# The first layer norm's normalisation moved from VectorE to ScalarE, as a scale and a shift

## The chip, the cores and the metric

The kernel runs on one core of a Trainium2 chip. The metric is the device time of one execution in microseconds (us). The engines are TensorE (PE, and PEld for its weight loads), VectorE (DVE), ScalarE (ACT), GpSimd (POOL) and the sync engine (SP), which issues most DMAs. Each takes its own list of instructions in order, and they wait for one another with semaphores.

## The reference

One transformer layer on 2 x 1024 tokens of width 512, all in float32. Cut to what matters:

```python
def _layernorm(x, axis=-1, eps=1e-05):
    m = jnp.mean(x, axis=axis, keepdims=True)
    v = jnp.var(x, axis=axis, keepdims=True)
    return (x - m) / jnp.sqrt(v + eps)

x = _layernorm(x + attention(x))      # 16 heads of 32, low-rank additions to q, k, v, o
x = _layernorm(x + moe(x))            # 8 experts, the best one per token, capacity 256, and a shared expert
```

The change is in the first of the two layer norms, between the attention's output projection and the router and experts.

## The kernel before

The kernel computes float32 products as three products of a high and a low half (`hi`, `lo`), so every operand of TensorE is first split: ScalarE writes the high half (a rounding copy) and VectorE the rest (a subtraction).

The attention takes until about 634 us. Then comes the stage of the change, over 16 tiles of 128 tokens by 512, in four groups of four (`i`, with `t = 4*i + j`), and after it the shared expert, the routing and the experts.

For a tile t of this stage:

- SP loads the attention columns (`at_in`, L535) and the input rows (`xr`, L538). GpSimd adds the output bias to `xr` (L693).
- ScalarE makes the high half of `at_in` (`at_hi`, L1267), VectorE the low half (`at_rest`, L1548). TensorE multiplies with `Wo` (`project`, L993, which is recorded at L751).
- VectorE adds the residual to the product in `rows[:, t]` (L1587) and takes the statistics (L1591).
- After four tiles, VectorE aggregates and adds epsilon (L1568, L1570), ScalarE takes the root (`root`, L1291), and VectorE forms the reciprocal with one Newton step (`scales`, L1575 to L1579) and normalises the four tiles in place (L1627).
- TensorE transposes the four normalised tiles (`turn_x1`, L1001, recorded at L758), after the projection of the next group; ScalarE takes the high half of the transposed tile (`x1_hi`, L1167) and VectorE the rest (`x1_rest`, L1420).

The order is written out by hand in each engine's list. On VectorE a group i is: the four tiles, each with the low half for the tile two further on; aggregation; the rest of the transposed tiles of group i-1; the scales; the four normalisations; for i = 1, 2, 3 the low half of one chunk of the shared expert's weights (`conv(13, ...)`, L1601). On ScalarE a group i is: the high halves for tiles 4i+2 to 4i+5; a copy of logits for i = 2, 3; the high halves of the transposed tiles of group i-1; the root; for i = 1, 2, 3 the high half of that same chunk (L1300). On TensorE: the projection of the group, logits of group i-2 for i = 2, 3, the transposes of group i-1; at the end the transposes of group 3, then the first product of the shared expert. SP loads tiles in order, but has loads of weight chunks between them: before tile 12's columns it waits for the semaphore `conv13`, which VectorE's L1601 increments, and loads the chunk (13, 2).

The second layer norm, at the kernel's end, already works with a scale and a shift: VectorE computes them (L1749, L1750) and ScalarE applies them (L1387).

Of the kernel before, what the change touches and what calls it, by code (L numbers as in the profile page):

```python
# [23 lines left out]
F32 = mybir.dt.float32  # L24
# [3 lines left out]
ACT = mybir.ActivationFunctionType  # L28
ALU = mybir.AluOpType
AX = mybir.AxisListType  # L30

P = 128
# [200 lines left out]
def emit(nc, ctx, x, W, bias, bo, Bm, Am, Wg, W1, W3, W2, sw1, sw3, sw2, out):  # L233
    sems = {}

    def sem(name):
        if name not in sems:
            sems[name] = ctx.enter_context(nc.semaphore(name))
        return sems[name]
# [66 lines left out]
    early = Arena(nc, region, small_at - V_BYTES)  # L306
# [7 lines left out]
    wg_raw = early("wg_raw", [P, DC, E], F32)  # L314
    st6 = early("st6", [P, 4, 6], F32)
    mv = early("mv", [P, 4, 2], F32)
    ln_v, ln_s, ln_r, ln_t = (early(f"ln_{n}", [P, 4], F32) for n in "vsrt")
    mid = Arena(nc, small_at - V_BYTES, overlay)
    raw2 = [mid(f"raw2_{i}", [P, D], F32) for i in range(2)]
    r3 = {n: mid(f"r3_{n}", [P, NT, E], F32) for n in ("lg", "d", "ex", "c", "oh", "s0", "s1", "io")}  # L320
# [7 lines left out]
    ln2_v, ln2_s, ln2_r, ln2_t, ln2_scale, ln2_shift = (mid(f"ln2_{n}", [P, NT], F32) for n in ("v", "s", "r", "t", "scale", "shift"))  # L328
    gate_sb = mid("gate_sb", [P, E * CAP // P], F32)
    wide = Arena(nc, overlay, sum_at)  # L330
    rows = wide("rows", [P, NT, D], F32)
# [827 lines left out]
    def _(ac):  # L1159
        ACTV = nc.scalar.activation  # L1160
# [58 lines left out]
        i, dc = 4, 0  # L1219
# [42 lines left out]
        def at_hi(t):  # L1262

            ac.wait_ge(sem(f"at_ld{t % 4}"), t // 4 * 16 + 16)
            if t >= 2:
                ac.wait_ge(sem("o_full"), t - 1)
            ACTV(at[t % 2][0][:], at_in[t % 4][:], ACT.Identity).then_inc(sem("at_hi"), 1)  # L1267
# [13 lines left out]
        def x1_hi(i):  # L1281
            for j in range(4):
                turned(i, j, x1_bank(4 * i + j), ("x1_t", 0), "x1_hi")

        def take_logits(i):
            ac.wait_ge(sem("lg_full"), i + 1)
            ACTV(lgT[:, i * 512:(i + 1) * 512], bank[6 + i % 2][0:E, :], ACT.Copy).then_inc(sem("lg_ev"), 1)

        def root(k, name):
            ac.wait_ge(sem(name + "_var"), k)  # L1290
            ACTV(ln_s[:], ln_v[:], ACT.Sqrt).then_inc(sem(name + "_root"), 1)  # L1291


        def conv(kind, c, sets, need):

            if kind == 13:
                ac.wait_ge(sem(f"raw13_ld{c % 2}"), sets * 96 + 32 * (c // 2 + 1))
                if need is not None:
                    ac.wait_ge(sem("ab_full"), need + (c + 1))
                ACTV(w13[c][0][:], raw13[c % 2][:, 0:1 + (c < FC - 1)], ACT.Identity).then_inc(sem("conv13_hi"), 1)  # L1300
            else:
                ac.wait_ge(sem(f"raw2_ld{c % 2}"), sets * (8 * (6 + 2 * (c % 2))) + 16 * (c // 2 + 1 + (c == FC - 1)))
                if need is not None:
                    ac.wait_ge(sem("used2"), need + (c + 3))
                ACTV(w2[0][:, c], raw2[c % 2][:], ACT.Identity).then_inc(sem("conv2_hi"), 1)

        def step(c, q, width):

            r, p0 = c % 2, tail(c)
            ac.wait_ge(sem("ab_full"), q + (c + 1))  # L1310
            ac.wait_ge(sem("hid_lo"), q + (c + 1))
            ACTV(sa[r][p0:P, 0:width], bank[2 * r][0:P - p0, 0:width], ACT.Silu).then_inc(sem("sa_rdy"), 1)  # L1312
            ac.wait_ge(sem("h_done"), q + (c + 3))
            ac.wait_ge(sem("used2"), q + (c + 1))
            ACTV(hid[r][0][p0:P, 0:width], sa[r][p0:P, 0:width], ACT.Identity).then_inc(sem("hid_hi"), 1)  # L1315
# [21 lines left out]
        for i in range(4):  # L1337
            for t in range(4 * i + 2, min(4 * i + 6, NT)):
                at_hi(t)
            if i >= 2:  # L1340
                take_logits(i - 2)
            if i:
                x1_hi(i - 1)
            root(i + 1, "ln1")
            if i in FIRST_PROJ:
                conv(13, FIRST_PROJ[i], 0, None)
        x1_hi(3)
# [37 lines left out]
        def normalised(start, stop):  # L1385
            for t in range(start, stop):
                ACTV(rows[:, t], rows[:, t], ACT.Identity, scale=ln2_scale[:, t:t + 1],  # L1387
                     bias=ln2_shift[:, t:t + 1]).then_inc(sem("out_rdy"), 1)

        def root2(k, start, stop):  # L1390
            ac.wait_ge(sem("ln2_var"), k)
            ACTV(ln2_s[:, start:stop], ln2_v[:, start:stop], ACT.Sqrt).then_inc(sem("ln2_root"), 1)

        for c in range(FC):
            step(c, (E + 3) * FC, 512)
            if c == 3:
                root2(1, 0, 12)
            if c == 4:
                ac.wait_ge(sem("ln2_shift"), 1)
                normalised(0, 8)  # L1400
        normalised(8, 12)
        root2(2, 12, NT)
        ac.wait_ge(sem("ln2_shift"), 2)
        normalised(12, NT)


# [1 line left out]
    def _(ve):  # L1408
        TT, TS, RED = nc.vector.tensor_tensor, nc.vector.tensor_scalar, nc.vector.tensor_reduce
# [88 lines left out]
        n, i, t, dc = 0, 4, V_FIRST, 0  # L1498
# [66 lines left out]
        def variances(link, name):  # L1565

            for j in range(4):
                ins = nc.vector.bn_aggr(mv[:, j], st6[:, j])  # L1568
            link(ins)
            TS(ln_v[:], mv[:, :, 1], EPS, None, ALU.add).then_inc(sem(name + "_var"), 1)  # L1570

        def scales(link, k, name, out=ln_r):

            ve.wait_ge(sem(name + "_root"), k)
            link(nc.vector.reciprocal(ln_r[:], ln_s[:]))  # L1575
            link(TT(ln_t[:], ln_r[:], ln_r[:], ALU.mult))
            link(TT(ln_t[:], ln_t[:], ln_v[:], ALU.mult))
            link(TS(ln_t[:], ln_t[:], -0.5, 1.5, ALU.mult, ALU.add))
            link(TT(out[:], ln_r[:], ln_t[:], ALU.mult))  # L1579

        def tiles(i, link):

            for j in range(4):
                t = 4 * i + j
                ve.wait_ge(sem("o_full"), t + 1)
                ve.wait_ge(sem("xb_rdy"), t + 1)
                TT(rows[:, t], bank[(0, 1, 4)[t % 3]], xr[j][:], ALU.add).then_inc(sem("y_done"), 1)  # L1587
                if t + 2 < NT:
                    at_rest(t + 2)
                ve.wait_ge(sem("y_done"), t + 1)  # L1590
                link(nc.vector.bn_stats(st6[:, j], rows[:, t]))  # L1591

        def x1_rest(i):
            for j in range(4):
                turned(i, j, x1_bank(4 * i + j), "x1_hi", "x1_lo")

        def conv(kind, c, sets):

            if kind == 13:
                ve.wait_ge(sem("conv13_hi"), sets * FC + (c + 1))  # L1600
                TT(w13[c][1][:], raw13[c % 2][:, 0:1 + (c < FC - 1)], f32(w13[c][0][:]), ALU.subtract).then_inc(sem("conv13"), 1)  # L1601
            else:
                ve.wait_ge(sem("conv2_hi"), sets * FC + (c + 1))
                p0 = tail(c)
                TT(w2[1][p0:P, c], raw2[c % 2][p0:P, :], f32(w2[0][p0:P, c]), ALU.subtract).then_inc(sem("conv2"), 1)  # L1605
# [12 lines left out]
        link = Chain(ve, sem("ln1_chain"))  # L1618
        for i in range(4):
            tiles(i, link)  # L1620
            variances(link, "ln1")
            if i:
                x1_rest(i - 1)
            scales(link, i + 1, "ln1")
            for j in range(4):
                t = 4 * i + j
                TS(rows[:, t], rows[:, t], mv[:, j, 0:1], ln_r[:, j:j + 1], ALU.subtract, ALU.mult).then_inc(sem("x1_rdy"), 1)  # L1627
            if i in FIRST_PROJ:
                conv(13, FIRST_PROJ[i], 0)
        x1_rest(3)  # L1630
# [6 lines left out]
        def by_t(b, k=0):  # L1637
            return b[:, k * P:(k + 1) * P].rearrange("p (t e) -> p t e", e=E)

        link = Chain(ve, sem("rt_chain"))  # L1640
# [9 lines left out]
                                            op0=ALU.is_equal, op1=ALU.mult))  # L1650
# [12 lines left out]
        for k in (1, 2, 4, 8):  # L1663
# [9 lines left out]
                                            op0=ALU.mult, op1=ALU.add))  # L1673
# [53 lines left out]
        link = Chain(ve, sem("ln2_chain"))  # L1727
# [14 lines left out]
        def scales2(k, start, stop):  # L1742
            r, tt, v, scale = (x[:, start:stop] for x in (ln2_r, ln2_t, ln2_v, ln2_scale))
            ve.wait_ge(sem("ln2_root"), k)
            link(nc.vector.reciprocal(r, ln2_s[:, start:stop]))
            link(TT(tt, r, r, ALU.mult))
            link(TT(tt, tt, v, ALU.mult))
            link(TS(tt, tt, -0.5, 1.5, ALU.mult, ALU.add))
            link(TT(scale, r, tt, ALU.mult))  # L1749
            nc.vector.scalar_tensor_tensor(out=ln2_shift[:, start:stop], in0=mv2[:, start:stop, 0], scalar=-1.0, in1=scale,  # L1750
                                           op0=ALU.mult, op1=ALU.mult).then_inc(sem("ln2_shift"), 1)

        for c in range(FC):
            step(c, (E + 3) * FC, 512)
# [6 lines left out]
        for t in range(12, NT):  # L1761
# [4 lines left out]
            stats(t, t + 1)  # L1766
        variances2(12, NT)
        scales2(2, 12, NT)


# [32 lines left out]
```

## Time and profile before

| what | value |
|---|---|
| median of 3 runs | 1122.74 us (1121.78 to 1123.65) |
| the profiled execution, its own time | 1124.97 us |
| its span in the trace | 1123.3 us |
| PE busy | 1064.0 us (95%) |
| DVE busy | 725.5 us (65%) |
| ACT busy | 552.1 us (49%) |
| POOL busy | 472.9 us (42%) |

The span is what the trace covers; the device time has 1.7 us around it. Busy times are sums over the engine's instructions. In the rows of a timeline, the first two numbers are the start and the duration in us, and brackets at the end give how long the engine had been idle and what released it. A row with "x4" merges four instructions of one line.

### The profile page before, as it was taken

The page shows a single profiled execution, that of the slowest core. Times are in us where ns is not written, and L with a number is a line of the kernel's source. Part 1 is how long each engine was busy: PE and PEld are TensorE (multiplying, and loading weights), DVE is VectorE, ACT ScalarE, POOL GpSimd, SP SyncE. Part 2 cuts the span into 40 slices and gives each one's busy share as a digit, 9 for nine tenths or more (in the row PEclk, how much of TensorE's full clock was granted, in tenths as well). Part 3 has the DMA queues.
Part 4 walks back from the last instruction along what each step waited for, and adds up shares of the span by engine and source line. Part 5 has one row for each costly group of instructions (what it writes and reads, how often), then busy time and mean ns, then how long its engine had stood idle before and what let it go on. Part 6 is the DMA issues. An engine that isn't in the chain of part 4 may idle for free.

```text
span 1123.3 us, 16277 instructions
## 1 busy us (share of the span) xinstructions
PE 1064.0 (95%) x5710; PEld 738.1 (66%) x5710; DVE 725.5 (65%) x1202; ACT 552.1 (49%) x969; POOL 472.9 (42%) x269
## 2 busy tenths in 40 slices
PE   4899999999999999999999969899999999999995
PEld 3777556465564645555443557678899999998884
DVE  3337967878777787877775478453376666664163
ACT  4220465656566565656657422342356655663125
POOL 2100476884848678484867632047000000003500
PEclk9899999999999999999999989899999999999997
DMA  8556341402423142232356243043357677775604
GB/s 271 198 177 188 101 115 39 95 29 63 116 60 93 39 95 65 58 85 57 95 136 194 83 142 113 19 163 85 85 171 237 211 227 230 222 209 119 93 1 150
DMA packets 154533, 138.40 MB, mean 123 GB/s; under 512 B 43537, under 2 KB 119569, under 8 KB 154208
## 3 DMA queue, kind: packets, MB, share of 16 engines
q1 hardware_dynamic: 147808, 121.58, 38.7%
q0 software_dynamic: 6656, 15.93, 5.1%
q8 instruction: 40, 0.66, 0.2%
q14 instruction: 29, 0.24, 0.1%
HBM read 81.56 MB, written 31.47 MB: 101 GB/s over the span
## 4 chain that ended last, share of the span: by engine, by line
PE 80%; DVE 9%; ACT 3%; DMA 3%; issue 2%; SPq 2%; POOL 0%; ACTq 0%; DVEq 0%
PE bank L751 20%; PE bank L897 12%; PE bank L910 11%; PE bank L845 10%; PE bank L1028 10%; PE bank L833 8%; PE bank L922 4%; PE bank L806 3%; DVE mx L1483 2%; PE bank L758 1%; DMA raw<-in_L_ffn_W_dram 1%; DVE xTlo L1420 1%; DMA at_in<-attn_d 1%; ACT rows L1387 1%; PE bank L784 1%
## 5 line engine op out<-in xcount | busy, mean ns | idle before, releaser
L1483 DVE TENSOR_REDUCE mx<-bank 128x1 f32<-128x512 f32 x512 | 323.5, 680 | 99.1 <-PE bank L845 96.9
L1245 ACT ACTIVATE prob<-bank 128x512 f32<-128x512 f32 x512 | 289.6, 597 | 192.9 <-PE bank L897 179.6
L678 POOL TENSOR_TENSOR psum<-psum,prob 128x1024 f32<-128x1024 f32 x122 | 286.9, 2392 | 0.0
L897 PE MATMUL bank<-Qs,Ks 97*128 97x512 f32 x512 | 208.2, 423 | 1.9 <-DMA Qs<-mrow 0.9
L845 PE MATMUL bank<-Ks,Qs 96*128 96x512 f32 x512 | 188.4, 407 | 2.6 <-DVE mx L1483 1.3
L897 PEld LDWEIGHTS bank<-Qs,Ks 97*128 97x128 f32 x512 | 95.4, 188 | 112.6 <-ACT prob L1245 74.0
L678 POOL TENSOR_TENSOR psum<-prob,prob 128x1024 f32<-128x1024 f32 x32 | 75.8, 2388 | 139.0 <-PE bank L922 135.3
L910 PE MATMUL bank<-prob,V 128*32 128x512 f32 x1024 | 132.6, 606 | 0.0
L845 PEld LDWEIGHTS bank<-Ks,Qs 96*128 96x128 f32 x512 | 96.4, 189 | 44.5 <-DVE mx L1483 13.9
L730 POOL DMA_DIRECT2D oe_d<-oe_sb x16 | 8.8, 548 | 231.4 <-ACT oe_sb L1367 230.4
L833 PE MATMUL bank<-xThi,Wsl 128*128 128x512 f32 x256 | 98.0, 398 | 1.2 <-DVE plane_klo L1473 0.8
L1612 DVE TENSOR_TENSOR sa<-bank,sa 128x256 f32<-128x256 f32 (+1 forms) x72 | 36.7, 510 | 76.7 <-ACT sa L1312 76.1
L1312 ACT ACTIVATE sa<-bank 128x256 f32<-128x256 f32 (+1 forms) x72 | 32.4, 450 | 103.8 <-PE bank L751 100.9
L1536 DVE RECIPROCAL bank<-bank 128x128 f32<-128x128 f32 x64 | 60.2, 951 | 14.8 <-PE bank L922 14.8
L910 PEld LDWEIGHTS bank<-prob,V 128*32 128x32 f32 x1024 | 24.1, 109 | 52.5 <-issue 35.6
L833 PEld LDWEIGHTS bank<-xThi,Wsl 128*128 128x128 f32 x256 | 48.3, 189 | 13.1 <-issue 1.0
L648 POOL DMA_DIRECT2D v_d<-v_sb x16 | 8.9, 559 | 103.8 <-DVE v_sb L1451 103.8
L833 PE MATMUL bank<-xTlo,Wsl 128*128 128x512 f32 x128 | 50.4, 394 | 0.0
L1605 DVE TENSOR_TENSOR w2lo<-raw,w2hi 128x512 fp32r<-128x512 f32 (+1 forms) x60 | 41.0, 685 | 0.9
L1028 PE MATMUL bank<-w2hi,hid1hi 128*128 128x512 f32 x96 | 38.3, 399 | 2.8 <-DVE hid1hi L1615 2.8
L1028 PE MATMUL bank<-w2hi,hid0hi 128*128 128x512 f32 x96 | 39.4, 410 | 1.2 <-DVE hid0lo L1615 0.4
L1315 ACT ACTIVATE hid0hi<-sa 128x256 fp32r<-128x256 f32 (+1 forms) x36 | 17.6, 490 | 45.2 <-DVE sa L1612 45.2
(222 smaller groups left out, 2111.9 us busy)
## 6 DMA issues: line engine op xcount, KB each, us to landing
raw<-in_L_ffn_W_dram SPq DMA_DIRECT2D x120, 256.0 KB, 3.6
Ks<-plane_khi SPq DMA_DIRECT2D x64, 128.0 KB, 2.3
Qs<-plane_qhi SPq DMA_DIRECT2D x64, 128.0 KB, 2.3
raw<-in_L_ffn_sw_dram SPq DMA_DIRECT2D x30, 256.0 KB, 3.6
xin<-in_L_attn_x_dram SPq DMA_DIRECT2D x16, 256.0 KB, 5.3
v_d<-v_sb POOLq DMA_DIRECT2D x16, 256.0 KB, 3.3
Wsl<-wt_d SPq DMA_DIRECT2D x16, 256.0 KB, 4.0
Ks<-plane_klo SPq DMA_DIRECT2D x32, 128.0 KB, 2.3
```

Source lines behind the costliest of these rows:

```text
L678: po.tensor_tensor(psum[:, pr], (prob[0] if kc == 1 else psum)[:, pr], prob[kc % RING][:, pr], ALU.add).then_inc(sem("sum_done"), 1)
L751: mm = nc.tensor.matmul(dst, lhs(a, dc), rhs(b, dc), start=dc == 0 and k == 0, stop=dc == DC - 1 and k == 2)
L833: mm = nc.tensor.matmul(pj, Wsl[:, m, a, dc, :], xT[p][:, dc, cols], start=dc == 0 and k == 0, stop=dc == DC - 1 and k == 2)
L845: mm = nc.tensor.matmul(dst, Qs[b][0:96, hh, q0:q0 + P], Ks[b][0:96, hh, part * 512:part * 512 + 512], start=True, stop=True)
L897: nc.tensor.matmul(score_at(v, i), Ks[v.b][0:97, hh, kc * P:(kc + 1) * P], Qs[v.b][0:97, hh, v.hf * HALF:(v.hf + 1) * HALF], start=True, s ...
L910: mm = nc.tensor.matmul(ov[hh * HD:(hh + 1) * HD, :], V[b][:, kc % KC, hh * HD:(hh + 1) * HD], prob[kc % RING][:, hh, :], start=kc == 0, s ...
L922: mm = nc.tensor.matmul(dn[hh * HD:(hh + 1) * HD, :], ones32[:], part[:, hh, :], start=summed[n] == 1, stop=summed[n] == KC - SUMS[n] + 1)
L1028: mm = nc.tensor.matmul(bank[4 + i], hid[c % 2][a][:, i * P:(i + 1) * P], w2[p][:, c, :], start=c == 0 and k == 0, stop=c == FC - 1 and k ...
L1245: ACTV(prob[kc % RING][:, hh, :], score_at(v, i), ACT.Exp, scale=SCALE).then_inc(sem("exp_done"), 1)
L1483: ins = RED(mx[(hf + ahead) % 2][:, 4 * hh + qt, part:part + 1], src, AX.X, ALU.max)
L1536: nc.vector.reciprocal(part, part).then_inc(sem("rden"), 1)
L1605: TT(w2[1][p0:P, c], raw2[c % 2][p0:P, :], f32(w2[0][p0:P, c]), ALU.subtract).then_inc(sem("conv2"), 1)
```

## The change

The normalisation `(x - mean) * r` becomes `x * scale + shift` with `scale = r` and `shift = -mean * r`. VectorE writes scale and shift into two new 128x4 tiles and signals `ln_shift`; ScalarE waits for it and applies them with four ACTIVATEs per group, in place, right after the root and ahead of its weight chunk. As the tiles of scale and shift are used again by the next group, the scales wait for the previous group's four normalised tiles. The semaphore `ln2_shift` of the second layer norm becomes the same `ln_shift`, with its counts going on at 5 and 6.

```diff
-    ln_v, ln_s, ln_r, ln_t = (early(f"ln_{n}", [P, 4], F32) for n in "vsrt")
+    ln_v, ln_s, ln_r, ln_t, ln_scale, ln_shift = (early(f"ln_{n}", [P, 4], F32) for n in ("v", "s", "r", "t", "scale", "shift"))
...
+        def x1(i):
+            ac.wait_ge(sem("ln_shift"), i + 1)
+            for j in range(4):
+                t = 4 * i + j
+                ACTV(rows[:, t], rows[:, t], ACT.Identity, scale=ln_scale[:, j:j + 1],
+                     bias=ln_shift[:, j:j + 1]).then_inc(sem("x1_rdy"), 1)
...
             root(i + 1, "ln1")
+            x1(i)
             if i in FIRST_PROJ:
                 conv(13, FIRST_PROJ[i], 0, None)
...
-                ac.wait_ge(sem("ln2_shift"), 1)
+                ac.wait_ge(sem("ln_shift"), 5)
...
-        ac.wait_ge(sem("ln2_shift"), 2)
+        ac.wait_ge(sem("ln_shift"), 6)
...
             ve.wait_ge(sem(name + "_root"), k)
+            ve.wait_ge(sem("x1_rdy"), 4 * (k - 1))
...
-            link(TT(out[:], ln_r[:], ln_t[:], ALU.mult))
+            link(TT(ln_scale[:], ln_r[:], ln_t[:], ALU.mult))
+            nc.vector.scalar_tensor_tensor(out=ln_shift[:], in0=mv[:, :, 0], scalar=-1.0, in1=ln_scale[:],
+                                           op0=ALU.mult, op1=ALU.mult).then_inc(sem("ln_shift"), 1)
...
             scales(link, i + 1, "ln1")
-            for j in range(4):
-                t = 4 * i + j
-                TS(rows[:, t], rows[:, t], mv[:, j, 0:1], ln_r[:, j:j + 1], ALU.subtract, ALU.mult).then_inc(sem("x1_rdy"), 1)
             if i in FIRST_PROJ:
                 conv(13, FIRST_PROJ[i], 0)
```

## Rows read from the trace of the kernel before

**Rows 1.** The page's first part: the span, and TensorE's busy time.
```profile
span 1123.3 us, 16277 instructions
...
PE 1064.0 (95%) x5710; PEld 738.1 (66%) x5710; DVE 725.5 (65%) x1202; ACT 552.1 (49%) x969; POOL 472.9 (42%) x269
```

**Rows 2.** Busy time by stretch: length, PE, PEld, DVE, ACT, POOL, clock, DMA, GB/s.
```profile
656.30:676.50 20.20, 14.29 (x54) 11.73 (x55) 15.70 (x32) 4.47 (x8) 5.10 (x4) 0.75 0.31 92
676.50:695.40 18.90, 17.29 (x83) 13.96 (x82) 15.46 (x33) 6.94 (x12) 6.00 (x4) 1.00 0.46 139
```

**Rows 3.** The chain of waits in order of time: start, duration, piece.
```profile
676.57 1.13 DVE w_0lo L1601
...
711.83 1.91 DVE rows L1627 x4
...
717.56 14.85 PE bank L751 x60
```

**Rows 4.** Timeline of VectorE, first group.
```profile
654.42 1.92 DVE L1627 TENSOR_SCALAR rows<-rows,mv,ln_r 128x512 f32<-128x512 f32 x4
...
656.86 0.68 DVE L1548 TENSOR_TENSOR at0lo<-at_in,at0hi 128x512 fp32r<-128x512 f32 x1
```

**Rows 5.** Timeline of VectorE, second group, and the last group's first low half.
```profile
668.48 1.23 DVE L1570 TENSOR_SCALAR ln_v<-mv 128x4 f32<-128x4 f32 x1
...
674.65 1.92 DVE L1627 TENSOR_SCALAR rows<-rows,mv,ln_r 128x512 f32<-128x512 f32 x4
676.48 1.22 DVE L1601 TENSOR_TENSOR w_0lo<-raw,w_0hi 128x1024 fp32r<-128x1024 f32 x1
677.62 0.69 DVE L1587 TENSOR_TENSOR rows<-bank,xr 128x512 f32<-128x512 f32 x1
...
714.79 1.28 DVE L1420 TENSOR_TENSOR xTlo<-bank,xThi 128x512 fp32r<-128x512 f32 x2
```

**Rows 6.** Timeline of TensorE: tiles 4, 6, 7, a transpose, tiles 10, 14, the last transposes.
```profile
648.47 0.50 PE L751 MATMUL bank<-wohi,at0hi 128*128 128x512 f32 x1 [2.40 <-DVE at0lo L1548]
...
657.59 0.50 PE L751 MATMUL bank<-wohi,at0hi 128*128 128x512 f32 x1 [3.15 <-DVE at0lo L1548]
...
662.03 0.40 PE L751 MATMUL bank<-wohi,at1hi 128*128 128x512 f32 x1
...
664.78 1.03 PE L758 MATMUL bank<-ident,rows 128*128 128x128 f32 x8
...
678.96 0.50 PE L751 MATMUL bank<-wohi,at0hi 128*128 128x512 f32 x1
...
697.82 0.50 PE L751 MATMUL bank<-wohi,at0hi 128*128 128x512 f32 x1 [1.12 <-DVE at0lo L1548]
...
712.43 1.88 PE L758 MATMUL bank<-ident,rows 128*128 128x128 f32 x8 [2.87 <-DVE rows L1627]
```

**Rows 7.** Timeline of ScalarE in the same stage.
```profile
652.74 0.62 ACT L1267 ACTIVATE at0hi<-at_in 128x512 fp32r<-128x512 f32 x1
...
673.01 1.05 ACT L1300 ACTIVATE w_0hi<-raw 128x1024 fp32r<-128x1024 f32 x1
676.50 0.63 ACT L1267 ACTIVATE at0hi<-at_in 128x512 fp32r<-128x512 f32 x1 [2.45 <-PE bank L751]
...
713.49 0.60 ACT L1167 ACTIVATE xThi<-bank 128x512 fp32r<-128x512 f32 x1 [2.26 <-PE bank L758]
```

**Rows 8.** Lines L1291 and L1387 (ns min/median/max), and both engines' timelines at the end.
```profile
L1291 ACT ACT_TABLE_LOAD  x1: 1283/1283/1283, 649.1 to 649.1; - x1
...
L1387 ACT ACTIVATE rows<-rows,ln_shift,ln_scale x16: 797/800/812, 1100.2 to 1120.1; 128x512 f32<-128x512 f32 x16
...
1117.77 0.16 DVE L1750 SCALAR_TENSOR_TENSOR ln_shift<-mv,ln_scale 128x4 f32<-128x4 f32 x1
1117.96 2.92 ACT L1387 ACTIVATE rows<-rows,ln_shift,ln_scale 128x512 f32<-128x512 f32 x4 [1.24 <-DVE ln_shift L1750]
```

**Rows 9.** Timeline of the sync engine: the load of tile 12's attention columns.
```profile
678.70 0.51 SPq L535 DMA_DIRECT2D at_in<-attn_d  x1
```

More of the change, by code:

```diff
@@ L1570, in variances, with scales @@
             TS(ln_v[:], mv[:, :, 1], EPS, None, ALU.add).then_inc(sem(name + "_var"), 1)
-        def scales(link, k, name, out=ln_r):
+        def scales(link, k, name):
             ve.wait_ge(sem(name + "_root"), k)
+            ve.wait_ge(sem("x1_rdy"), 4 * (k - 1))
             link(nc.vector.reciprocal(ln_r[:], ln_s[:]))
@@ L1750, in scales2 @@
             nc.vector.scalar_tensor_tensor(out=ln2_shift[:, start:stop], in0=mv2[:, start:stop, 0], scalar=-1.0, in1=scale,
-                                           op0=ALU.mult, op1=ALU.mult).then_inc(sem("ln2_shift"), 1)
+                                           op0=ALU.mult, op1=ALU.mult).then_inc(sem("ln_shift"), 1)
         for c in range(FC):
```

## The prediction

> **What bounds the kernel now.** I read the page first: TensorE is busy for 95% of a span of 1123.3 us [rows 1], so whatever lengthens TensorE's waits lengthens the kernel, and a saving elsewhere counts only if TensorE was waiting for it. The change touches one stage, from about 634 to 724 us, in which the attention output is projected, normalised and transposed. There the stage table shows that no engine is full: from 676.5 to 695.4 us TensorE works 17.29 of 18.90 us, VectorE 15.46 and ScalarE only 6.94 [rows 2]. A look at shares alone would say: move work from VectorE to ScalarE. So the next view is the chain of waits, which follows VectorE here through the conversion of a weight chunk that stands right behind the four normalising instructions, and in the last group through those four themselves [rows 3]. VectorE's place in the order of work is what matters. The last views are the timelines of the engines, which show who waits for whom.
>
> Call S the moment at which VectorE has the scale of four tiles ready. Before, the four subtract-and-multiply instructions start there: 654.42 us for the first group [rows 4], 674.65 for the second [rows 5]. In the first group, the subtraction that makes the low half for tile 6 starts at 656.86, S + 2.44 [rows 4], and TensorE, idle for 3.15 us, starts tile 6 at 657.59 [rows 6]. In the other three groups the low half of a weight chunk (L1601) comes next: 676.48, S + 1.83, and then tile 8's residual sum at 677.62 [rows 5]. ScalarE is ahead of all this: it made the high half for tile 6 at 652.74, and the high half of the weight chunk at 673.01, 1.64 us before S, then it idled for 2.45 us until 676.50 [rows 7]. That head start is what the change spends.
>
> **What is removed and added on VectorE.** Four L1627 instructions per group go (16 in all): from 674.65 to 676.48 is 1.83 us of VectorE's time [rows 5]. One small scalar_tensor_tensor per group comes; the same operation in the second layer norm, at the same 128x4, takes 0.16 us, and ScalarE starts 0.19 us after its start [rows 8]. Its bound upwards is a small VectorE operation that ran into a GpSimd addition, 1.23 us [rows 5]. GpSimd is not adding at any of the four S, so I take 0.16. The added wait of the scales on the previous four normalised tiles costs nothing: those were ready some 18 us before. The renamed semaphore of the second layer norm and the two 128x4 tiles cost nothing either: same instructions, same places.
>
> **What is added on ScalarE.** Four ACTIVATEs per group with scale and bias read from tiles. The tail of the kernel runs exactly this form, 800 ns each over 16, and four of them in 2.92 us [rows 8]. So successive starts are 0.71 apart, and what stands behind them starts 4 x 0.71 = 2.83 us after the first (the bound upwards is 2.92). The bound downwards is the cheap form: a 0.63 us ACTIVATE from SBUF with constant factors [rows 7]; at four in 2.1 us each group would cost 0.7 less. I take the exact form. No table load comes with it: the stage has one, in front of the first root [rows 8], and the constant-factor ACTIVATEs follow the roots without another [rows 7].
>
> What is queued behind is the point. ScalarE takes its instructions in order, so it now stands at the wait for the shift and runs the four before the work that VectorE needs next.
>
> First group: ScalarE starts at S + 0.19, is free at S + 3.02, makes tile 6's high half in 0.63 and VectorE subtracts from S + 3.70 (0.05 for the signal) instead of S + 2.44. That is **+1.26 us** for TensorE's start of tile 6. Before, tile 6 ran partly at the lower clock: it took 657.59 to 662.03, 4.44 us, and tile 7 664.78 - 662.03 = 2.75 us [rows 6], with a mean granted clock of 0.75 in that stretch [rows 2]. If the clock returns at the same moment, a later start has less of the work in the slow part. The slow part lost 1.69 us; I estimate that 0.46 of the 1.26 comes back so, and take **+0.8**, between 0.7 and 1.26. VectorE's own head start (the residual sum of tile 4 is 1.75 us earlier) buys nothing, since its next instruction waits for tile 6's high half.
>
> Second, third and fourth group: ScalarE's conversion of the chunk, 1.05 us [rows 7], now follows the four. VectorE's half of it can start at S + 0.19 + 2.83 + 1.05 + 0.04 = S + 4.11 instead of S + 1.83: **+2.28 us each, 6.84 for three**. Is there cover? In the second group the low half for tile 10 follows tile 8's residual sum and ends at 677.62 + 0.60 + 0.68 = 678.90 [rows 4, 5]; TensorE takes it up at 678.96, without having been idle [rows 6]. That is a cover of 0.06 us, so none. The sync queue does not absorb it either: the load of the next weight chunk waits for L1601, and the load of tile 12's attention columns is queued behind that load; it went out at 678.70 [rows 9] and goes out later by the same amount, so VectorE's wait for that transfer moves too. In the third group TensorE already waited 1.12 us for tile 14 [rows 6]. In the fourth, the first high half of the last four transposed tiles (713.49 on ScalarE [rows 7]) and L1601 in front of its low half (714.79 on VectorE [rows 5]) both come behind the chunk on their queues, while TensorE waits.
>
> Nothing behind the stage gives it back: from 717.56 us the chain is 60 products in a row on TensorE [rows 3], and everything it needs follows from it or was loaded early.
>
> **The clock.** Rows show what TensorE did before its granted clock was low: idle stretches of 3.15 and 2.87 us stood before work at 1.2 GHz, stretches of 2.40 and 1.12 us before work at 2.4 GHz [rows 6]. The change makes two more long ones: about 2.3 to 2.7 us before tile 10, and 1.12 + 2.28 = 3.4 us before tile 14. The second is longer than both that ended at the low clock, and behind it VectorE already waits for TensorE, so I charge one such slow part, **+1.7** (the 1.69 above). The first lies in between; behind it is the transfer wait, which hides most of it, so I take 0, bounds 0 and 1.7.
>
> **Sum.** 0.8 + 6.84 + 1.7 = +9.3 us. The profiled execution took 1124.97 us with a span of 1123.3, and so becomes 1134.3; it lies 2.2 above the median of 1122.74, to which I add the same: **1132.0 us**. Bounds: without the clock +7.6, and with the cheap ACTIVATE 4 x 0.7 less, +4.8 or 1127.5; upwards 1.26 for the first group and two slow parts, 1.26 + 6.84 + 3.4 = +11.5 or 1134.2, and 0.3 for the unknown spread.
>
> The Trainium skill has a rule against this change: "ScalarE: Activation LUTs", section "Rules for kernel authors", gives multiplications and additions to VectorE. The trace agrees in direction: 541 ns was the price there and 800 ns is the price here. Read as a price per instruction alone, the rule would make it some 16 x (0.71 - 0.46) = +4 us; that the sum is twice this comes from the order of the queues, of which the rule says nothing.
>
> **Rivals.**
> A, faster: VectorE is the bound and ScalarE is half idle. VectorE gets back 1.83 - 0.08 = 1.75 us four times, 7.0 in all: 1115.7 us. It holds only if what ScalarE has behind the four isn't what VectorE wants next, in the first group and at the three chunks. At the chunks, the point of balance is where 0.19 + 4x + 1.05 + 0.04 = 1.83, or x = 0.14 us per instruction; the row says 0.71. For it: the low share of ScalarE [rows 2]. I give 3%. "SBUF — State Buffer" of the Trainium skill, section "Who interferes with whom", would add to it: the removed form of instruction can keep GpSimd from its port. That relief would change no time here, as no GpSimd addition overlaps the four in any group.
>
> B, hidden: the longer waits fall into slack that the inferred releasers don't show (the transfer of the attention columns, TensorE's queue), and no more than the first group's 0.8 and some of the last is left: +2 us or less, 1123 to 1125. Against it is the 0.06 us of cover. 5%.
>
> C, the ACTIVATE is cheap in this place or a part is hidden: +2.3 to +5, 1125 to 1127.5. 14%.
>
> D, more than I count: both new idle stretches cost a slow part and the late conversions push the weight loads behind other traffic, or the ACTIVATE needs a table load in each group (1.28 us each, +5): above 1134.5. 10%. That the change doesn't do what it says is possible only in that last sense; the order of the instructions is explicit.
>
> **How the numbers follow.** The forecast has 68%, A 3, B 5, C 14, D 10. The measurement can tell about 0.2%, 2.2 us, from no change. So: faster 0.03, same 0.05, slower 0.92. The range goes from 1127.5 to 1134.5; outside lie C, B, A and D, of which C's upper part reaches just inside.
>
> **What would show it.** VectorE idle before L1601 with ScalarE's conversion as the releaser, some 3 us each, three times. ScalarE's four in 2.9 us, starting 0.19 after the shift. TensorE idle about 4.4 us before tile 6 and 3.4 before tile 14, and the long row of products (717.56 us before) later by 8 to 10 us. Wrong would be: that row beginning no later than 719, or four normalising ACTIVATEs done in less than 2 us.

## The result and the profile after

| what | before | after |
|---|---|---|
| median | 1122.26 us (4 runs, 1120.36 to 1123.65) | 1134.89 us (4 runs, 1130.6 to 1136.76) |
| the profiled execution | 1124.97 us, span 1123.3 | 1136.76 us, span 1135.1 |
| ratio | | 1.0119, 95% interval 1.0089 to 1.0148 |

The change makes the kernel about 1.2% slower, 13 us. The forecast of slower was right; 1134.89 lies 0.4 us above the range, and of +12.6 us the forecast had +9.3. Executions of one kernel differ by some microseconds, and the profiled one of the kernel before is 2.7 us above its median (after: 1.9), so a difference between two traces can be a microsecond or more off the difference between the medians.

The page after the change, its first part. It answers to [rows 1]:

```profile
span 1135.1 us, 16285 instructions
...
PE 1068.2 (94%) x5710; PEld 741.2 (65%) x5710; DVE 721.5 (64%) x1190; ACT 562.7 (50%) x985; POOL 472.3 (42%) x269
```

VectorE has 4 us less to do, ScalarE 11 more, and the span is 12 longer: no engine's share says so, the places do. Busy time by stretch, columns as in [rows 2]; the first row covers about the same work as the first row there:

```profile
656.30:676.50 20.20, 13.23 (x47) 10.77 (x48) 14.12 (x26) 4.65 (x10) 5.07 (x4) 0.68 0.26 79
676.50:695.40 18.90, 15.66 (x63) 12.22 (x61) 12.52 (x20) 7.84 (x12) 5.50 (x4) 0.89 0.46 139
```

From 676.5 to 695.4 us TensorE ran 63 products and transposes instead of 83, and its mean granted clock was 0.89 instead of 1.00.

The timeline of ScalarE after the change, first two groups, which answers to [rows 7]:

```profile
653.46 2.93 ACT L1298 ACTIVATE rows<-rows,ln_shift,ln_scale 128x512 f32<-128x512 f32 x4 [1.79 <-DVE ln_shift L1590]
656.30 0.61 ACT L1267 ACTIVATE at0hi<-at_in 128x512 fp32r<-128x512 f32 x1
...
676.60 2.93 ACT L1298 ACTIVATE rows<-rows,ln_shift,ln_scale 128x512 f32<-128x512 f32 x4 [1.74 <-DVE ln_shift L1590]
679.44 1.05 ACT L1308 ACTIVATE w_0hi<-raw 128x1024 fp32r<-128x1024 f32 x1
```

ScalarE now stands 1.8 us at the wait, works 2.93, and only then does what VectorE needs next. In [rows 7] the high half for tile 6 came at 652.74 and that of the chunk before the normalisation. The other side, VectorE, which answers to [rows 4] and [rows 5]:

```profile
653.27 0.16 DVE L1590 SCALAR_TENSOR_TENSOR ln_shift<-mv,ln_scale 128x4 f32<-128x4 f32 x1
653.35 0.69 DVE L1599 TENSOR_TENSOR rows<-bank,xr 128x512 f32<-128x512 f32 x1
656.94 1.78 DVE L1557 TENSOR_TENSOR at0lo<-at_in,at0hi 128x512 fp32r<-128x512 f32 x1 [2.90 <-ACT at0hi L1267]
...
676.40 0.17 DVE L1590 SCALAR_TENSOR_TENSOR ln_shift<-mv,ln_scale 128x4 f32<-128x4 f32 x1
680.51 1.23 DVE L1613 TENSOR_TENSOR w_0lo<-raw,w_0hi 128x1024 fp32r<-128x1024 f32 x1 [3.95 <-ACT w_0hi L1308]
```

With S the start of the small operation for the shift, the low half of the chunk starts at 680.51 - 676.40 = S + 4.11 (1.83 before), and the low half for tile 6 at S + 3.67 (2.44 before). The brackets name ScalarE. One thing is new: that low half took 1.78 us, not 0.68. And TensorE, which answers to [rows 6]:

```profile
658.77 0.79 PE L751 MATMUL bank<-wohi,at0hi 128*128 128x512 f32 x1 [5.48 <-DVE at0lo L1557]
...
663.89 0.39 PE L751 MATMUL bank<-wohi,at1hi 128*128 128x512 f32 x1
...
683.00 0.50 PE L751 MATMUL bank<-wohi,at0hi 128*128 128x512 f32 x1 [1.86 <-DVE at0lo L1557]
...
687.33 0.50 PE L751 MATMUL bank<-wohi,at1hi 128*128 128x512 f32 x1
...
705.84 0.80 PE L751 MATMUL bank<-wohi,at0hi 128*128 128x512 f32 x1 [3.40 <-DVE at0lo L1557]
...
711.13 0.54 PE L751 MATMUL bank<-wohi,at1hi 128*128 128x512 f32 x1
```

The ends of tiles 10 and 14 before (their starts are in [rows 6]):

```profile
681.85 0.39 PE L751 MATMUL bank<-wohi,at1hi 128*128 128x512 f32 x1
...
700.68 0.39 PE L751 MATMUL bank<-wohi,at1hi 128*128 128x512 f32 x1
```

Each pair of rows brackets one tile's product: tile 6 takes 5.12 us (4.44 before), tile 10 takes 4.33 (2.89 before) and tile 14 takes 5.29 (2.86 before). Tiles 6 and 14 begin at the low level, 1.2 GHz, products 0.63 long instead of 0.39; tile 10 falls to it after the fourth product.

**Where the time went.** Measured from VectorE's first low half of the stage (631.88 us before, 630.78 after) to the last transposes (715.62 and 728.53), the stage takes 83.74 and 97.75 us, 14.0 more. It is made up of:

| stretch | us longer | what changed in it |
|---|---|---|
| first S to the low half of tile 6 | 1.2 | order: S + 3.67, not S + 2.44 |
| that low half | 1.1 | 1.78 us long, not 0.68 |
| tile 6 on TensorE | 0.7 | more of it at 1.2 GHz |
| S to the chunk's low half, three times | 6.8 | order: S + 4.11, not S + 1.83 |
| start of tile 10 (683.00) to the third S (699.26) | 1.7 | tile 10 at 1.2 GHz, and a small VectorE operation stretched |
| tiles 14, 15 and the logits on TensorE | 2.6 | tile 14 at 1.2 GHz throughout |
| rest | -0.1 | |

The stretched small operation of the fifth row is the addition of epsilon in the third group. A GpSimd addition had started 0.10 us ahead of it:

```profile
693.73 1.26 POOL L693 TENSOR_TENSOR xr<-xr,bo_bc 128x512 f32<-128x512 f32 x1 [1.51 <-DMA xr<-in_L_attn_x_dram]
693.83 1.20 DVE L1579 TENSOR_SCALAR ln_v<-mv 128x4 f32<-128x4 f32 x1
```

In the kernel before, the same operation was not stretched:

```profile
689.11 0.17 DVE L1570 TENSOR_SCALAR ln_v<-mv 128x4 f32<-128x4 f32 x1
```

How the 1.7 us divide can be estimated from e2, in which tile 10 is as slow (4.45 us) but this operation takes 0.17. The stretch takes 14.56 us before, 15.62 in e2 and 16.26 in the change: about 1.1 is the clock and 0.6 the stretched operation. So of the 14.0 us some 8.1 are the order, 4.4 the low clock and 1.7 VectorE instructions held up by GpSimd. Tile 8 also takes 0.27 longer (4.48, not 4.21), but tile 10 starts no later for it.

Before the stage 1.1 us is gained in code that nobody changed, and after it another 1.1, so that the span grows by 11.8.

### The profile page after: what moved, and what is told of

It is laid out like the page before. It is cut to its first block, busy times and chain, and to the rows that moved or that the text cites. A ratio compares the mean times of both kernels' runs of the same rounds, so it can differ in the third digit from the quotient of the medians.

```text
span 1135.1 us, 16285 instructions
## 1 busy us (share of the span) xinstructions
PE 1068.2 (94%) x5710; PEld 741.2 (65%) x5710; DVE 721.5 (64%) x1190; ACT 562.7 (50%) x985; POOL 472.3 (42%) x269
## 4 chain that ended last, share of the span: by engine, by line
PE 81%; DVE 8%; ACT 4%; issue 2%; DMA 2%; SPq 2%; ACTq 0%; DVEq 0%
PE bank L751 21%; PE bank L897 12%; PE bank L910 11%; PE bank L845 10%; PE bank L1028 9%; PE bank L833 8%; PE bank L922 4%; PE bank L806 3%; DVE mx L1492 2%; PE bank L758 1%; DMA raw<-in_L_ffn_W_dram 1%; ACT rows L1298 1%; SPq L397 1%; DVE xTlo L1429 1%; ACT rows L1396 1%
```

## The experiments

All are the changed kernel with one edit, if nothing else is said. Ratios are to the kernel before on the same chip. The experiments ran on three chips, on which the kernel before took 1121.19 us (e0 to e3), 1120.13 (e4 to e8) and 1139.03 (e9, e10); so ratios are compared.

| run | edit | median us | ratio (95% interval) |
|---|---|---|---|
| e0 | none | 1134.77 | 1.0126 (1.0106 to 1.0147) |
| e1 | chunk ahead of the normalisation | 1124.34 | 1.0030 (1.0016 to 1.0044) |
| e2 | one row load held back | 1131.09 | 1.0094 (1.0064 to 1.0123) |
| e3 | extra products in three waits | 1131.06 | 1.0083 (1.0062 to 1.0104) |
| e4 | constant factors | 1128.14 | 1.0068 (1.0043 to 1.0092) |
| e6 | normalisation in ScalarE's gaps | 1116.70 | 0.9973 (0.9957 to 0.9990) |
| e7 | e6, last group on VectorE | 1117.49 | 0.9972 (0.9955 to 0.9988) |
| e8 | e7, extra products in a fourth wait | 1116.09 | 0.9953 (0.9933 to 0.9972) |
| e9 | e2 and e3 together | 1147.00 | 1.0067 (1.0042 to 1.0093) |
| e10 | kernel before, ScalarE only waits | 1143.88 | 1.0044 (1.0028 to 1.0060) |

### e0: the change again

> The changed kernel once more, timed in the same rounds as the experiments beside it. Both theories expect what was measured: 1131 to 1137 us, 10 to 14 above the kernel before. The distance from S (the last small VectorE operation of a group) to the low half of the weight chunk should be 4.11 us again, whatever the total is; what differs between executions should be only the length of TensorE's stretches at the low clock.

1134.77 us. The row that shows the chunk's low half starts at 678.86, its S at 674.75: S + 4.11 again. The slowdown repeats, and so do the stretches of the table: 16.26 us from tile 10 to the third S, 5.28 for tile 14.

### e1: the chunk first

```diff
             root(i + 1, "ln1")
-            x1(i)
             if i in FIRST_PROJ:
                 conv(13, FIRST_PROJ[i], 0, None)
+            x1(i)
```

> ScalarE converts its weight chunk before it waits for the shift. Theory 1 (the order on ScalarE costs, not the price of the ACTIVATEs): the low half of the chunk starts within 0.3 us of S instead of 4.11, the low half for tile 10 at about S + 3.7 us (before 3.57), and three times 2.28 us go together with the low-clock stretches behind tiles 10 and 14: 1124 to 1127 us, against 1134.9 for the change. Theory 2 (ScalarE's instructions are just dearer, 16 x 0.25 us, and the rest is the clock): the total falls by less than 3 us, to 1132 or more.

VectorE in this run:

```profile
674.38 0.16 DVE L1590 SCALAR_TENSOR_TENSOR ln_shift<-mv,ln_scale 128x4 f32<-128x4 f32 x1
674.46 1.22 DVE L1613 TENSOR_TENSOR w_0lo<-raw,w_0hi 128x1024 fp32r<-128x1024 f32 x1
...
678.06 0.69 DVE L1557 TENSOR_TENSOR at0lo<-at_in,at0hi 128x512 fp32r<-128x512 f32 x1 [1.74 <-ACT at0hi L1267]
```

The chunk's low half follows S at once, and the low half for tile 10 comes at S + 3.68. The same ACTIVATEs at the same price, two lines swapped: the ratio falls from 1.0126 to 1.0030, 10.4 us between the medians. That decides for the order (theory 1) and against the price (theory 2). 10.4 is more than the 6.8 of the three chunks. The rest goes with the clock: in the profiled executions, 13 products of the stage (L751, up to the last transposes) were 0.6 us long or more before, 37 in the change and in e0, and 17 in e1. e1 is still some 3 us slower than the kernel before: the first group has the change's order and its stretched low half (1.58 us).

### e2: the row load held back

The low half for tile 6 was stretched. GpSimd's timeline in the change has an addition that starts 0.03 us ahead of it:

```profile
656.91 1.26 POOL L693 TENSOR_TENSOR xr<-xr,bo_bc 128x512 f32<-128x512 f32 x1 [4.30 <-DMA xr<-in_L_attn_x_dram]
```

Before, this addition came at 659.59, behind the low half (656.86). The change itself moved it: VectorE's residual sum of tile 4 comes 1.75 us earlier against S, this frees a buffer, and the sync queue issues the row load of tile 8 at 654.06 instead of 656.96.

```diff
             if t >= 4:
-                sp.wait_ge(sem("y_done"), t - 3)
+                sp.wait_ge(sem("y_done"), t - 3 + (t == 8))
```

> The sync queue holds the load of tile 8's input rows back until tile 5 has its residual (one wait raised by one), so that GpSimd's addition no longer stands where VectorE makes tile 6's low half. If that collision is what stretches the low half from 0.69 to 1.78 us, it takes 0.7 us again and TensorE starts tile 6 about 1.1 us earlier; total 1 to 3 us below the change (the upper end if a low-clock stretch shortens too). If something else stretches it, it stays at 1.7 us and the total within 1 us.

```profile
656.53 0.69 DVE L1557 TENSOR_TENSOR at0lo<-at_in,at0hi 128x512 fp32r<-128x512 f32 x1 [2.91 <-ACT at0hi L1267]
...
661.20 1.29 POOL L693 TENSOR_TENSOR xr<-xr,bo_bc 128x512 f32<-128x512 f32 x1 [9.00 <-DMA xr<-in_L_attn_x_dram]
```

With GpSimd out of the way the same instruction takes 0.69 us, at the same S + 3.67. So the collision and its 0.7 to 1.1 us are shown in the trace (1.43 us long in e0, 1.78 in the change). The median is 3.7 us lower, above the expected 1 to 3, but its runs go from 1126.46 to 1137.02 and the intervals overlap, so the medians don't settle that surplus. The trace shows where it can come from. Held back by one load, GpSimd also left alone two more VectorE instructions of the second group that it had stretched in the change: the low half for tile 9 (0.69 us, 1.70 in the change) and the addition of epsilon (0.17, 1.11 in the change). And tile 14 ran at full clock, 2.6 us less up to the next transposes, which no part of this edit aims at. The Trainium skill states this under "SBUF — State Buffer", section "Who interferes with whom": a VectorE instruction with two SBUF inputs contends with a GpSimd instruction that reads SBUF, and the later one waits. The trace agrees: the residual sum at 647.91 us, with one input from PSUM, kept its 0.69 us beside GpSimd's additions in this stage. The addition of epsilon, which has one input tile, was held up all the same (1.20 us).

This run also holds a warning about the clock:

```profile
700.78 0.50 PE L751 MATMUL bank<-wohi,at0hi 128*128 128x512 f32 x1 [3.37 <-DVE at0lo L1557]
701.12 0.40 PE L751 MATMUL bank<-wolo,at0hi 128*128 128x512 f32 x1
```

Tile 14 starts after an idle stretch of 3.37 us at full clock; in the change it started after 3.40 at the low one.

### e3: extra products in the waits

```diff
             for t in range(4 * i, 4 * i + 4):
+                for _ in range({6: 14, 10: 8, 14: 14}.get(t, 0)):
+                    nc.tensor.matmul(bank[5], wo[0][:, 0, 0:P], wo[0][:, 0, :], start=True, stop=True)
                 pe.wait_ge(sem("at_lo"), t + 1)
```

> TensorE runs 14, 8 and 14 extra products into an unused bank while it would wait for tiles 6, 10 and 14 (3.2, 1.8 and 3.2 us of work inside waits of 5.5, 1.9 and 3.4 us). If the low clock behind those waits carries 3 to 5 us of the slowdown, tiles 6, 10 and 14 take 2.75 us each instead of 4.4 to 5.3 and the total falls by 3 to 5 us, to 1130 to 1132. If the clock is only a companion of the waits and hides in them, the total stays within 1 us of the change, 1134 to 1136, or gets worse by the extra products.

TensorE in this run:

```profile
660.69 0.50 PE L751 MATMUL bank<-wohi,at0hi 128*128 128x512 f32 x1 [0.71 <-DVE at0lo L1559]
...
666.27 1.03 PE L758 MATMUL bank<-ident,rows 128*128 128x128 f32 x8
...
703.77 0.50 PE L751 MATMUL bank<-wohi,at0hi 128*128 128x512 f32 x1 [0.20 <-DVE at0lo L1559]
...
712.14 1.04 PE L758 MATMUL bank<-ident,rows 128*128 128x128 f32 x8
```

Tiles 6 and 7 together take 5.58 us up to the transposes (7.89 in the change), tiles 14, 15 and the logits 8.37 (10.98). With more work on TensorE the median falls by 3.7 us, inside the 3 to 5 that were expected if the clock costs. The low clock was a real part of the cost and not hidden in the waits. How much is less sure: the profiled execution is the slowest of the six (1135.31), and in it the addition of epsilon in the third group took 0.17 us too, so a part of the gain may be that.

### e4: constant factors

```diff
-                ACTV(rows[:, t], rows[:, t], ACT.Identity, scale=ln_scale[:, j:j + 1],
-                     bias=ln_shift[:, j:j + 1]).then_inc(sem("x1_rdy"), 1)
+                ACTV(rows[:, t], rows[:, t], ACT.Identity).then_inc(sem("x1_rdy"), 1)
```

> The four ACTIVATEs copy the rows without scale and bias (the normalisation is left out, so the routing of the tokens changes too), in the order of the change. It takes the price of reading the two factors out: 0.63 us instead of 0.80 each, 0.18 less from start to start, 0.7 us per group. Theory 1 (each microsecond that ScalarE is longer at this place comes out at the end, with some low clock on top): S to the chunk's low half 3.4 us instead of 4.11, total 2 to 4 us below the change, 1131 to 1133. Theory 2 (ScalarE's price is most of the slowdown): down to 1128 or less.

```profile
L1298 ACT ACTIVATE rows<-rows x16: 613/615/636, 653.3 to 715.8; 128x512 f32<-128x512 f32 x16
```

This kernel leaves the normalisation out. 0.615 us instead of 0.801, and S + 3.38 to the chunk's low half. The two factors cost 186 ns. The Trainium skill, "ScalarE: Activation LUTs", section "What ACT_TABLE_LOAD costs", gives some 93 ns for each such operand; the trace agrees. The median, 1128.14, is 6.6 us below the change: between the two expectations, and only 0.14 above what theory 2 asked for. But the direct part is 4 x 0.73 = 2.9. In the trace the stage is 8.6 us shorter than in the change. 2.6 of it are tiles 14 and 15 and the logits, at full clock here, behind a wait of 2.63. The remaining 3.1 come with the collisions and tile 6: the low half for tile 6 (656.09) was ahead of GpSimd's addition (656.66) and took 0.69 us, and both additions of epsilon took 0.17. So the run does not say that the price is most of the slowdown; how the side effects share what is not direct, it can't tell.

### e6, e7: the normalisation where ScalarE is idle

In e6 ScalarE normalises group i-1 behind the first two high halves of group i, and the chunk stays ahead:

```diff
             for t in range(4 * i + 2, min(4 * i + 6, NT)):
+                if i and t == 4 * i + 4:
+                    x1(i - 1)
                 at_hi(t)
+            if i == 3:
+                x1(2)
...
             root(i + 1, "ln1")
-            x1(i)
             if i in FIRST_PROJ:
                 conv(13, FIRST_PROJ[i], 0, None)
+            if i == 3:
+                x1(3)
```

> ScalarE normalises the first three groups later, in the gap behind the high halves of the next two tiles, the chunk's high half stays ahead; the fourth group right after the chunk. If the order is all that was wrong with the change, VectorE's freed 1.75 us now come through: the low half for tile 6 at S + 0.7 us instead of 2.44, TensorE's waits before tiles 6 and 14 shrink by 1.7 and 1.1 us, the fourth group loses 0.7: 1117 to 1120 us, 1 to 5 below the kernel before. If there is another cost in ScalarE's form, it is 1122 or more.

```profile
653.44 0.16 DVE L1595 SCALAR_TENSOR_TENSOR ln_shift<-mv,ln_scale 128x4 f32<-128x4 f32 x1
654.13 0.68 DVE L1562 TENSOR_TENSOR at0lo<-at_in,at0hi 128x512 fp32r<-128x512 f32 x1
...
667.55 0.16 DVE L1595 SCALAR_TENSOR_TENSOR ln_shift<-mv,ln_scale 128x4 f32<-128x4 f32 x1
667.63 1.22 DVE L1618 TENSOR_TENSOR w_0lo<-raw,w_0hi 128x1024 fp32r<-128x1024 f32 x1
669.37 0.68 DVE L1562 TENSOR_TENSOR at0lo<-at_in,at0hi 128x512 fp32r<-128x512 f32 x1
```

Low half for tile 6 at S + 0.69, and TensorE's waits before tiles 6, 10 and 14 are gone. The median is 1116.70 (1117 to 1120 was expected), ratio 0.9973 (0.9957 to 0.9990): this version beats both kernels. Moving the work to ScalarE was sound; the place in its queue was not.

> The same, but the fourth group, for which TensorE waits at once, is normalised by VectorE. The first row of it is ready at S + 0.54 instead of S + 0.99 and ScalarE is free for the transposed tiles: 0.5 to 1 us less than the run before it, 1116 to 1119 us. If the fourth group's wait hides the difference, no change.

```diff
             scales(link, i + 1, "ln1")
+            if i == 3:
+                for j in range(4):
+                    t = 4 * i + j
+                    TS(rows[:, t], rows[:, t], mv[:, j, 0:1], ln_scale[:, j:j + 1], ALU.subtract, ALU.mult).then_inc(sem("x1_rdy"), 1)
```

In e7 the scales are followed, for the last group alone, by VectorE's old four instructions and ScalarE skips them. From S to the last transposes it is 705.34 - 701.47 = 3.87 us, in e6 705.81 - 701.33 = 4.48: 0.6 less in the traces, but the medians (1117.49, 1116.70) show no difference.

### e8: a fourth wait filled

```diff
+                if t == 2:
+                    for _ in range(18):
+                        nc.tensor.matmul(bank[5], wo[0][:, 0, 0:P], wo[0][:, 0, :], start=True, stop=True)
                 if t >= 2:
                     pe.wait_ge(sem("x1_lo"), t - 1)
```

> That kernel with 18 extra products on TensorE (about 4 us) inside its wait of 4.5 us in the middle of the first group's transposes. If the low clock behind that wait costs, tile 8 takes 2.75 us instead of 4.2 and the total falls by 1 to 2 us; if VectorE's work that follows hides it, no change or up to 0.5 us worse.

1116.09 us and 0.9953 (0.9933 to 0.9972), against 0.9972 (0.9955 to 0.9988) without it: lower, but inconclusive. The wait that it fills had itself shrunk to 2.54 us in e7, from the 4.5 that the expectation took from the change, and tile 8 behind it already ran at full clock there (2.81 us), so there was little to gain.

### e9: what is left without collision and low clock

> The change with both: the row load of tile 8 held back and the extra products before tiles 6, 10 and 14. What is left should be the order alone, 1.26 + 3 x 2.28 = 8.1 us, and the low clock where no extra products stand: 1127 to 1130 us. If the two savings overlap (a shorter wait before tile 6 has no low clock to lose), it is no better than either alone, 1131.

Ratio 1.0067 (1.0042 to 1.0093). Three products of the stage were slow. On the first chip the ratio would be 1122 x 0.0067 = 7.5 us over the kernel before, that is 1130, the upper end of what was expected, and near the 8.1 us of the order. It is no clean measure of the order, though. The kernel before has such side effects itself, and e9 removes these too: tile 6 takes 2.85 us (4.44 before), the low half for tile 9 0.69 (1.72) and the addition of epsilon in the second group 0.17 (1.23 in [rows 5]). In its trace the stage is 87.92 us, only 4.2 longer than the 83.74 of the kernel before, which was profiled on another chip.

### e10: the order alone

The kernel before, in which ScalarE waits for the normalised tiles and does nothing new:

```diff
             root(i + 1, "ln1")
+            ac.wait_ge(sem("x1_rdy"), 4 * i + 4)
             if i in FIRST_PROJ:
```

> The kernel before, with nothing moved: VectorE still normalises, but ScalarE waits for the four normalised tiles before it goes on to the chunk or to the next high halves. If it is the order that costs, the chunk's low half starts at S + 3.0 us instead of S + 1.83 (1.92 for the four, 0.04, 1.05 for the chunk's high half, 0.04), tile 6's low half at S + 2.65 instead of 2.44: 3 x 1.2 + 0.2 = 3.8 us and some low clock, 1124 to 1127 us. If the cost comes with the ACTIVATEs, it stays at the kernel before.

```profile
672.20 1.92 DVE L1628 TENSOR_SCALAR rows<-rows,mv,ln_r 128x512 f32<-128x512 f32 x4
675.25 1.22 DVE L1602 TENSOR_TENSOR w_0lo<-raw,w_0hi 128x1024 fp32r<-128x1024 f32 x1 [1.13 <-ACT w_0hi L1300]
```

S + 3.05, and 1.0044 (1.0028 to 1.0060): 5 us slower with no instruction moved and none added but the wait. Taking away ScalarE's head start costs by itself.

## Why the prediction was right or wrong

- **What bounds the stage, and the order of the queues:** right. S + 4.11 was forecast and measured to the hundredth, four ACTIVATEs took 2.93 us and started 0.19 to 0.20 after S. In the first group, S + 3.70 was forecast and 3.67 came. The 6.84 + 1.26 stand as 6.8 + 1.2; e1 and e10 bear them out from two sides, and e9's ratio agrees. That the transfer of tile 12's columns moves with L1601 was right as well: it went out at 682.74 instead of 678.70.
- **The clock:** right in kind, mis-sized. The step "I estimate that 0.46 of the 1.26 comes back" failed: tile 6 took 0.7 us longer, not 0.46 less. "The first lies in between ..., so I take 0" failed: tile 10 took 1.44 longer, and about 1.1 of it reached the next S. "I charge one such slow part, **+1.7**" was low: tiles 14 and 15 took 2.6 more, because the whole product of tile 14 ran at 1.2 GHz, while the 4.44 us of tile 6 that set the price had caught the clock's return. In the place of +1.24 net stood about +4.4.
- **A term that was missing:** 1.7 us in which VectorE was held up by GpSimd. "GpSimd is not adding at any of the four S" was true and did not help: the prediction priced this collision, at 1.23 us, for the operation at S alone. One addition came 3.6 us behind the first S, onto tile 6's low half (1.1 us); the change had moved it there. The step that failed is "VectorE's own head start ... buys nothing". It bought an earlier row load, and that landed on a path that counts. Another addition met the addition of epsilon in the third group (some 0.6 us).
- **Sum:** 14.0 us of the stage against 9.3, and more than the 11.5 of the upper bound. In the traces 2.2 of it came back outside the stage, in code that nobody changed; the medians moved by 12.6. So it is partly luck that the range ended only 0.4 short. The long row of products began at 730.47, 12.9 us later and not 8 to 10.
- **A sign that was misread:** VectorE's idle time before the chunk's low half was 3.95 us, three times, and not "some 3 us": S + 4.11 less the 0.16 of the small operation already said so. TensorE's wait before tile 10 was 1.86 and not 2.3 to 2.7, and the clock fell all the same.
- **Rival A** (faster) failed at the place that it named: x would have had to be under 0.14 us and was 0.71. Its reason, ScalarE's idle share, was good: e6 made a gain of 0.27% of it. B and C did not happen. **D** is nearest to what came: its bound of 1134.5 was passed, and both new idle stretches did cost low clock. It was not by table loads: there was none new.

## What to carry to other kernels

Before work is moved to the engine with the lower share, look at what stands behind the new place in its queue and who waits for that; if it is on the path, put the moved work further down, where the engine idles. The time by which an engine is ahead of the one that it feeds is worth something, even if it only idles in it: here the same four instructions per group cost 13 us in one place and gained 3 in another. And an engine that gets ahead starts its loads earlier: check what those will meet.

## What was not expected of the hardware

- An idle TensorE cost more than the wait. Of 14.0 us in the stage about 4.4 were products at 1.2 GHz behind longer waits, and filling three waits with useless products (e3) made the kernel 3.7 us faster.
- The length of a wait alone did not tell which level followed: 3.37 us and then full clock in e2, 3.40 us and then the low one in the change; in e4, 2.63 us before tile 14 and then full clock, 1.95 us before tile 10 and then the low one. Executions of one kernel differ: e2 took 1126.46 us at a mean granted clock of 0.981 and 1137.02 at 0.976.
- A VectorE subtraction with both inputs in SBUF took 1.78 instead of 0.69 us when a GpSimd addition had started 0.03 us before it. A VectorE addition on 128x4 elements, with one input tile, took 1.20 instead of 0.17 us when a GpSimd addition had started 0.10 us before it.
